# Transposed down products in three chunks of the last MoE stage: fp32r passes over split values instead of fp32 products

## The chip, the cores and the metric

The kernel runs on one core of one Trainium2 chip. The metric is the device time of one execution in microseconds. The kernel before takes 651.67 us, the median of three runs (651.1 to 653.26).

## What is computed

The input x holds 2 x 1024 tokens with 128 features. Six blocks are added to it one after another: a quantized FFN, a linear attention, the same FFN again, a mixture of experts (MoE), a causal softmax attention, and the same MoE a second time. Each block works on the layer-normed x. The change touches the last of them:

```
x = x + 0.5 * _L1_ffn_ref(_layernorm(x, axis=-1), ...)

logits = einsum('td,ed->te', x, router_w)          # 16 experts
top_w, top_i = top_k(softmax(logits), 2); top_w = top_w / sum(top_w)
dense_w = zeros((T, 16)).at[arange(T)[:, None], top_i].add(top_w)
for wg, wu, wd, cw in (Wg, Wu, Wd, dense_w.T):     # F = 64 each
    h = silu(x @ wg) * (x @ wu)
    acc = acc + cw[:, None] * (h @ wd)
shared = sigmoid(x @ shared_gate_w) * (silu(x @ Sg) * (x @ Su) @ Sd)   # FS = 256
```

All experts are computed for all tokens, and the weights of the experts not chosen are zero.

## The kernel before

**Units and chunks.** The 2048 tokens are cut into NC = 4 chunks of 512. The 16 x 64 expert columns and the 256 shared ones make NU = 10 units of 128 hidden columns. A MoE stage is a loop over 40 pairs of chunk and unit, numbered n = 0 to 39 in this text. Unit n of a chunk is u = n mod 10. `MOE0` is the first such stage and `MOE1` the last; both run the same code.

**What a unit does.** TensorE forms the gate and the up product of the unit (`gate_up`, L1325 to L1327): each is three fp32r passes of 512 columns over values that were split into a high and a low part (`mm3`), into banks 1 to 3 and 4 to 6 by turns. ScalarE takes Silu of the gate bank (L764, into `sg`). VectorE multiplies it with the up bank (L1130, into `su`) and that with the routing weights `gb` (L1134, into `hbuf`, three buffers by turns). Then TensorE does the down product of the unit: four products, one for each tile of 128 tokens, with the tile of `hbuf` as the stationary operand and 128 columns of the fp32 down weights `dw` as the moving one (L1545), summed over the ten units in bank 7 (`ACC`).

**Order on TensorE.** In step n of the loop in `moe` TensorE does gate_up(n), then at certain u the chunk's side work, then the down product of unit n - 2. The first three gate_up of the last stage are issued at the end of `causal`. gate_up(n) waits until `hbuf` of unit n - 3 is written, since it takes over that unit's banks.

**Side work of a chunk,** by u. At u = 1 TensorE transposes the next chunk's normed tokens into bank 0 (`ln`, L1333), ScalarE copies them out (L656), and VectorE adds the finished sum of the chunk before to x (`update`, L949) and splits the next chunk (`split`, L938 and L939). At u = 2 VectorE norms a later chunk (L925). At u = 3 TensorE forms the router's products (`route`, L1483 and L1485), which need that split, and VectorE picks the two experts. At u = 4 VectorE computes their weights (`weigh`). At u = 6 TensorE transposes them (`weights`, L1493), ScalarE copies them out (L752), and SyncE writes them to HBM. Bank 0 is passed from one of these users to the next: TensorE waits until the one before was drained (`t_take`).

**SyncE's queue.** For each chunk SyncE waits for the routing weights, writes them (L420), waits until they have landed, and then loads each unit's rows into `gb`, two loads a unit, 128 KB in all by the profile's count, four buffers by turns (L431). Behind the last of a chunk's loads stands the store of the finished chunk before (L436), which waits for `update`. The next chunk's L420 stands behind that store.

**GpSimd** has two short steps of the norm in this stage (L463, L464) and nothing else.

## Time and profile before

| | us |
|---|---|
| median of 3 runs | 651.67 |
| the profiled execution | 651.54 |
| its span | 649.8 |
| last MoE stage, from its first gate_up to the end of the span | 542.9 to 649.8 |
| TensorE busy over the span | 92% |
| VectorE busy over the span | 73% |
| GpSimd busy over the span | 25% |

The span is the time from the first to the last instruction; 1.7 us of the execution lie around it. TensorE carries the last stage nearly without a gap. The matmul records overlap each other, so that the duration of one record (0.40 us for 512 columns) is more than what it adds to the chain; the chain of work that ended last gives the distance from one to the next.

### The profile page before, as it was taken

Reading aid. Unit: us, or ns where it says so; the run is one execution under the profiler, and the core shown is the slowest. Engines: PE = TensorE matmul, PEld = TensorE weight load, DVE = VectorE, ACT = ScalarE, POOL = GpSimd, SP = SyncE. Lnnn points to the kernel's source line nnn. Section 1 sums busy time; section 2 is a strip of 40 time slices with the busy share of each in tenths; the row PEclk is TensorE's granted clock in tenths of the full one; section 3 lists DMA queues with packets and bytes.
Section 4 is the critical chain, followed back from the end, with each engine's and each line's share of the span. In section 5 each row is a group of like instructions: output and inputs, shape, how many; then the busy total and the mean of one; then the engine's idle time right before and its main releaser. Section 6 shows DMA issues by size and latency. Waiting matters only on the chain. (4 is left out here: it accounts for less than half of the span.)

```text
span 649.8 us, 12519 instructions
## 1 busy us (share of the span) xinstructions
PE 598.2 (92%) x4364; PEld 421.8 (65%) x4364; DVE 476.7 (73%) x1501; ACT 348.1 (54%) x713; POOL 161.4 (25%) x334
## 2 busy tenths in 40 slices
PE   6996879989999978999999999999999997999997
PEld 5785767878877956654535453545453545888887
DVE  5577866688787767879797878788879432976864
ACT  3855456323324552667676767676767674232321
POOL 7641534020024436722323121211120100000000
PEclk9999899999989995979999999999999999899999
DMA  8000000234322300000000000000000002333332
GB/s 297 6 2 0 2 1 0 68 101 131 116 75 79 94 1 2 1 2 1 2 2 2 1 3 1 1 2 2 1 3 1 2 2 68 99 121 126 115 126 71
DMA packets 18669, 27.98 MB, mean 43 GB/s; under 512 B 2984, under 2 KB 7208, under 8 KB 18608
## 3 DMA queue, kind: packets, MB, share of 16 engines
q1 hardware_dynamic: 17888, 25.85, 12.3%
q10 hardware_dynamic: 720, 1.34, 0.6%
q8 instruction: 35, 0.57, 0.4%
q14 instruction: 26, 0.21, 0.1%
HBM read 25.85 MB, written 1.33 MB: 42 GB/s over the span
## 5 line engine op out<-in xcount | busy, mean ns | idle before, releaser
L834 ACT ACTIVATE arena<-bank 128x512 f32<-128x512 f32 (+3 forms) x384 | 166.2, 496 | 66.5 <-PE bank L1669 46.1
L1700 PE MATMUL bank<-kza,qta 64*128 64x512 f32 (+3 forms) x432 | 139.5, 426 | 5.4 <-DVE work L1207 3.5
L1204 DVE CUSTOM_DVE_ANT_0 bank<-bank,mask_qk 128x512 f32<-128x512 f32 (+3 forms) x256 | 119.3, 518 | 32.1 <-PE bank L1700 31.7
L1657 PE MATMUL bank<-qtb,kza 64*128 64x512 f32 (+3 forms) x384 | 133.5, 407 | 4.4 <-ACT arena L834 1.6
L1700 PEld LDWEIGHTS bank<-kza,qta 64*128 64x128 f32 x432 | 69.3, 198 | 76.5 <-DVE work L1204 38.8
L764 ACT ACTIVATE work<-bank 128x512 f32<-128x512 f32 x80 | 47.7, 598 | 109.2 <-PE bank L1327 107.2
L1207 DVE TENSOR_REDUCE work<-bank 128x1 f32<-128x512 f32 x128 | 80.2, 683 | 15.5 <-PE bank L1700 15.5
L1545 PE MATMUL bank<-dw,work 128*128 128x128 f32 x640 | 86.2, 279 | 2.6 <-DVE work L1134 2.6
L1130 DVE TENSOR_TENSOR work<-work,bank 128x512 f32<-128x512 f32 x80 | 54.7, 683 | 44.3 <-PE bank L1327 39.8
L1545 PEld LDWEIGHTS bank<-dw,work 128*128 128x128 f32 x640 | 82.3, 193 | 7.2 <-issue 3.1
L1657 PEld LDWEIGHTS bank<-qtb,kza 64*128 64x128 f32 x384 | 64.6, 186 | 28.9 <-ACT arena L834 16.9
L1614 PE MATMUL bank<-arena 128*9 128x512 f32 (+3 forms) x768 | 80.8, 493 | 0.4 <-ACT arena L834 0.4
L1134 DVE TENSOR_TENSOR work<-work,kt 128x512 f32<-128x512 f32 x80 | 56.2, 703 | 5.1 <-DMA kt<-cw_rows 2.3
L463 POOL TENSOR_SCALAR rtmp<-mv 128x4 f32<-128x4 f32 x24 | 7.4, 308 | 170.5 <-DVE mv L913 170.1
L530 POOL CAST kza<-kt 32x512 fp32r<-32x512 f32 x48 | 29.1, 606 | 82.3 <-PE bank L1657 77.7
L1669 PE MATMUL bank<-identb,mask_kq 64*128 64x64 bf16 x512 | 47.6, 197 | 0.0
L925 DVE TENSOR_SCALAR hn<-x,mv,rs 128x128 f32<-128x128 f32 x96 | 29.0, 367 | 18.5 <-POOL rs L480 14.5
L1325 PE MATMUL bank<-qta,gh 128*128 128x512 f32 x80 | 38.4, 480 | 0.0
L1204 DVE DVE_READ_ACCUMULATOR2_ANT work<- 128x1 f32 x256 | 35.9, 140 | 0.0
L1377 PEld LDWEIGHTS bank<-work 128*128 128x128 f32 x256 | 32.4, 191 | 1.8 <-ACT work L674 0.3
L1377 PE MATMUL bank<-work 128*128 128x128 f32 x256 | 33.4, 275 | 0.1
L1669 PEld LDWEIGHTS bank<-identb,mask_kq 64*128 64x128 bf16 x512 | 24.6, 96 | 13.1 <-issue 8.2
(204 smaller groups left out, 1040.5 us busy)
## 6 DMA issues: line engine op xcount, KB each, us to landing
kt<-cw_rows SPq DMA_DIRECT2D x160, 128.0 KB, 2.9
x<-x_in SPq DMA_DIRECT2D x4, 256.0 KB, 7.4
y_out<-x SPq DMA_DIRECT2D x4, 256.0 KB, 3.2
arena<-gw_in SPq DMA_DIRECT2D x1, 640.0 KB, 9.6
arena<-uw_in SPq DMA_DIRECT2D x1, 640.0 KB, 8.6
dw<-dw_in SPq DMA_DIRECT2D x1, 640.0 KB, 9.5
work<-q_in SPq DMA_DIRECT2D x2, 256.0 KB, 8.0
arena<-const_in ACTq DMA_DIRECT2D x1, 400.0 KB, 6.7
```

The lines of the kernel that those rows point to most:

```text
L764: act.activation(sg[:, m % 2, :], bank[1 + m % 3][:, :], ACT.Silu).then_inc(sg_ready, 1)
L834: act.activation(pb[:, blk % 2, h, 0:w], s_bank(n)[:, 0:w], ACT.Exp, scale=SCALE).then_inc(p_ready, 1)
L1130: link(dve.tensor_tensor(su[:, m % 2, :], sg[:, m % 2, :], bank[4 + m % 3][:, :], ALU.mult))
L1134: dve.tensor_tensor(hbuf[:, m % 3, :], su[:, m % 2, :], gb[:, m % 4, :], ALU.mult)\
L1204: ins = dve.tensor_tensor_reduce(out=src, in0=src, in1=mask_qk[:, CW - w:], scale=1.0, scalar=-3e38, op0=ALU.add, op1=ALU.max, accum_out=dst)
L1207: ins = dve.tensor_reduce(dst, src, AX.X, ALU.max)
L1377: ins = pe.matmul(ACC[:, t * P:(t + 1) * P], hbuf[:, m % 4, t * P:(t + 1) * P], w2[:, k, :], start=False, stop=(k == FB - 1), skip_group_c ...
L1545: ins = pe.matmul(ACC[:, t * P:(t + 1) * P], hbuf[:, m % 3, t * P:(t + 1) * P], dw[:, u, :], start=(u == 0 and t == 0), stop=(u == NU - 1) ...
L1614: ins = pe.matmul(bank[7][h * SL:h * SL + HD + 1, CW - w:CW], va[:, b, j, g * GH + h, :], pb[:, blk % 2, h, 0:w], start=(j == 0), stop=Tru ...
L1657: ins = pe.matmul(s_bank(n)[:, 0:w], kz(s, h, j // CT)[pair(h), j % CT * P:(j % CT + 1) * P], qtb[pair(h), s % 2, (c + 1) * CW - w:(c + 1) ...
L1669: ins = pe.matmul(s_bank(n)[:, a * 2 * SL:(a + 1) * 2 * SL], mask_kq[r, a, :], identb[r, r], start=False, stop=True, skip_group_check=True)
L1700: ins = pe.matmul(a_bank(n)[:, 0:w], qta[pair(h), slot(b, g), i * P:(i + 1) * P], kz(s, h, half)[pair(h), 0:w], start=True, stop=True)
```

## The change

In the last MoE stage the down products of the first three chunks (units 0 to 29, `TURNED` = 30) take another form. The down weights become the stationary operand and the gated values the moving one, so that the sum arrives transposed, and both are split: three fp32r passes of 512 columns a unit in place of four fp32 products of 128 columns.

- `halves` splits the down weights once on VectorE (two passes of 128x1280), in step 7 of the causal stage.
- `high` copies each unit's gated values as their high part into `hhi` on ScalarE, behind the Silu of the next unit. GpSimd subtracts it from `hbuf` and writes the low part into `hlo`. Both have three buffers.
- `turned_down` does the three passes. It comes three steps behind gate_up instead of two, and so do the down products of the last chunk, whose form is the one of before.
- VectorE's write of `hbuf` for unit n waits until the low part of unit n - 3 is written, where it waited for the down product of that unit.
- At u = 2 of the next chunk ScalarE copies the transposed sum from bank 7 (`yturn`). At u = 7 TensorE transposes it back into bank 0 (`back`), and VectorE adds it to x from there. `update` of a chunk so moves from u = 1 to u = 7 of the next.
- The split weights, `hhi` and `hlo` lie in buffers of the causal stage, and the products that only keep TensorE busy at its end (`idle_product`) read another buffer.

```diff
@@ -617,7 +626,15 @@
             rstd(22)
-            rstd(23)
+            for n in range(TURNED):
+                pool.wait_ge(hhi_ready, n + 1)
+                if n >= 3:
+                    pool.wait_ge(down_done, 2 * NC * FB + NC * NU + n - 2)
+                pool.tensor_tensor(hlo[:, n % 3, :], hbuf[:, (NC * NU + n) % 3, :], hhi[:, n % 3, :].bitcast(F32),
+                                   ALU.subtract).then_inc(hlo_ready, 1)
+                if n == 4:
+                    rstd(23)
+                pool.wait_ge(hlo_ready, n + 1)
@@ -767,10 +784,24 @@
+                    if p == MOE1 and 1 <= n <= TURNED:
+                        high(n - 1)
+                    if p == MOE1 and c > 0 and u == 2:
+                        act.wait_ge(down_done, 2 * NC * FB + NC * NU + NU * c)
+                        if c > 1:
+                            act.wait_ge(back_full, c - 1)
+                        act.activation(yturn, ACC[:, :], ACT.Copy).then_inc(yt_copied, 1)
...
+            def high(n):
+
+                act.wait_ge(hm_ready, NC * NU + n + 1)
+                if n >= 3:
+                    act.wait_ge(down_done, 2 * NC * FB + NC * NU + n - 2)
+                act.activation(hhi[:, n % 3, :], hbuf[:, (NC * NU + n) % 3, :], ACT.Copy).then_inc(hhi_ready, 1)
@@ -1128,12 +1159,14 @@
-                    if m >= 3:
+                    if p == MOE1 and 3 <= n < TURNED + 3:
+                        dve.wait_ge(hlo_ready, n - 2)
+                    elif m >= 3:
                         dve.wait_ge(down_done, 2 * NC * FB + m - 2)
...
-                    if u == 1 and c > 0:
+                    if u == 1 and c > 0 and p == MOE0:
                         update(L - 1, 0.5)
@@ -1147,7 +1180,18 @@
+                    if p == MOE1 and c > 0 and u == 7:
+                        dve.wait_ge(back_full, c)
+                        update(L - 1, 0.5, T)
                 update(4 * p + 3, 0.5)
+
+            def halves():
...
+                link(dve.tensor_copy(dwh, flat))
+                dve.tensor_tensor(dwl, flat, dwh.bitcast(F32), ALU.subtract).then_inc(dws_ready, 1)
@@ -1518,7 +1564,8 @@
-                for n in range(NC * NU + 2):
+                lag = 3 if p == MOE1 else 2
+                for n in range(NC * NU + lag):
@@ -1535,16 +1582,42 @@
+                        if p == MOE1 and c > 0 and u == 7:
+                            back(L - 1, c)
+                    if p == MOE1 and lag <= n < TURNED + lag:
+                        turned_down(n - lag)
...
+            def turned_down(n):
...
+                if u == 0 and c > 0:
+                    pe.wait_ge(yt_copied, c)
+                pe.wait_ge(hlo_ready, n + 1)
+                f = slice(u * P, (u + 1) * P)
+                mm3(ACC[:, :], dwh[:, f], dwl[:, f], hhi[:, n % 3, :], hlo[:, n % 3, :], start=(u == 0),
+                    stop=(u == NU - 1)).then_inc(down_done, 1)
+
+            def back(L, c):
+
+                pe.wait_ge(yt_copied, c)
+                t_take(x_ready, L + 1)
+                for t in range(CT):
+                    ins = pe.transpose(T[:, t * P:(t + 1) * P], yturn[:, t * P:(t + 1) * P], ident[:, :])
+                ins.then_inc(back_full, 1)
```

TensorE at the start of the stage, before: the down product of unit 0 (bank 7 from `dw`) stands ahead of gate_up(3).

```order
L1333 MATMUL bank0<-identr,hn 128x128 x4
L1545 MATMUL bank7<-dw,work 128x128 x4
L1325 MATMUL bank2<-qta,gh 128x512
L1326 MATMUL bank2<-kt,gl 128x512
L1327 MATMUL bank2<-kt,gh 128x512
L1325 MATMUL bank5<-qta,vh 128x512
L1326 MATMUL bank5<-kt,vl 128x512
L1327 MATMUL bank5<-kt,vh 128x512
L1483 MATMUL bank0<-wr,kt 128x36
```

The same place after the change, where `mm3` is at L1371 to L1373 and the router's products at L1529:

```order
L1379 MATMUL bank0<-identr,hn 128x128 x4
L1371 MATMUL bank2<-qta,gh 128x512
L1372 MATMUL bank2<-kt,gl 128x512
L1373 MATMUL bank2<-kt,gh 128x512
L1371 MATMUL bank5<-qta,vh 128x512
L1372 MATMUL bank5<-kt,vl 128x512
L1373 MATMUL bank5<-kt,vh 128x512
L1529 MATMUL bank0<-wr,kt 128x36
```

The down product of unit 0 has moved behind the router's products, and nothing of unit 0 stands between the transposes and these any more.

ScalarE in chunk 1, before: Silu of the units (L764), the copy of the transposed tokens (L656) and the routing weights (L752).

```order
L752 ACTIVATE cwt<-bank 17x512
L764 ACTIVATE work<-bank 128x512 x5
L656 ACTIVATE ft<-bank 128x512
L764 ACTIVATE work<-bank 128x512 x3
L745 ACTIVATE th<-dd 128x8
```

After the change Silu is L781, the copy of the tokens L673, `high` L804 and the copy of the transposed sum L793:

```order
L781 ACTIVATE work<-bank 128x512
L673 ACTIVATE ft<-bank 128x512
L804 ACTIVATE kza<-work 128x512
L781 ACTIVATE work<-bank 128x512
L804 ACTIVATE kza<-work 128x512
L793 ACTIVATE work<-bank 128x512
L781 ACTIVATE work<-bank 128x512
```

Behind each Silu there is now one `high`, and at u = 2 also the copy of the sum, which waits for TensorE.

GpSimd in the last stage, before: the norm's two steps for chunks 2 and 3, then the end of the program.

```order
L463 TENSOR_SCALAR rtmp<-mv 128x4
L464 TENSOR_TENSOR rs<-rtmp,nhalf 128x4
L463 TENSOR_SCALAR rtmp<-mv 128x4
L464 TENSOR_TENSOR rs<-rtmp,nhalf 128x4
L176 UNCONDITIONAL_BRANCH
```

After the change (L472 and L473 are the norm's steps, L633 the subtraction):

```order
L472 TENSOR_SCALAR rtmp<-mv 128x4
L473 TENSOR_TENSOR rs<-rtmp,nhalf 128x4
L633 TENSOR_TENSOR qtb<-work,kza 128x512 x5
L472 TENSOR_SCALAR rtmp<-mv 128x4
L473 TENSOR_TENSOR rs<-rtmp,nhalf 128x4
L633 TENSOR_TENSOR qtb<-work,kza 128x512 x25
```

Thirty subtractions of 128x512 have been added, each with two tensor inputs in SBUF.

## Rows read from the trace of the kernel before

**Rows 1.** Windows over two chunks, from one `weights` on TensorE to the next.
```profile
core 0: us, PE busy (x) PEld busy (x) DVE busy (x) ACT busy (x) POOL busy (x), PEclk, DMA share, GB/s
564.25:588.80 24.55, 24.55 (x158) 21.79 (x157) 19.75 (x54) 7.37 (x13) 0.00 (x0) 1.00 0.33 117
588.80:613.35 24.55, 24.55 (x158) 21.80 (x157) 18.07 (x48) 7.37 (x13) 0.00 (x0) 1.00 0.39 120
```

**Rows 2.** Chain that ended last, in order of time: start us, us, what.
```profile
559.70 0.89 PE bank L1545 x8
560.59 0.23 PE bank L1325
...
564.25 0.44 PE bank L1493 x4
```

**Rows 3.** Groups by line, last stage: count, busy us, mean ns, idle before, releasers.
```profile
L764 ACT ACTIVATE work<-bank 128x512 f32<-128x512 f32 x40 | 23.8, 598 | 61.2 <-PE bank L1327 60.0 <-DVE work L1134 1.2
```

**Rows 4.** VectorE in order of time, start of the stage, and TensorE's wait there.
```profile
552.19 0.68 DVE L1130 TENSOR_TENSOR work<-work,bank 128x512 f32<-128x512 f32 x1
552.42 1.53 PE L1545 MATMUL bank<-dw,work 128*128 128x128 f32 x8 [1.86 <-DVE work L1134]
...
563.81 0.68 DVE L1130 TENSOR_TENSOR work<-work,bank 128x512 f32<-128x512 f32 x1
```

**Rows 5.** Window just behind that wait, columns as in rows 1.
```profile
553.00:556.50 3.50, 3.50 (x14) 2.92 (x13) 3.43 (x8) 0.60 (x1) 0.00 (x0) 0.51 0.54 150
```

**Rows 6.** VectorE in order of time, units 10 to 20.
```profile
573.90 0.69 DVE L1130 TENSOR_TENSOR work<-work,bank 128x512 f32<-128x512 f32 x1 [0.86 <-PE bank L1327]
...
580.49 1.11 DVE L925 TENSOR_SCALAR hn<-x,mv,rs 128x128 f32<-128x128 f32 x4
...
587.20 0.68 DVE L1130 TENSOR_TENSOR work<-work,bank 128x512 f32<-128x512 f32 x1
...
589.63 0.69 DVE L1134 TENSOR_TENSOR work<-work,kt 128x512 f32<-128x512 f32 x1
...
599.18 0.69 DVE L1134 TENSOR_TENSOR work<-work,kt 128x512 f32<-128x512 f32 x1
```

**Rows 7.** Groups by line and shape: GpSimd's passes over two SBUF tensors.
```profile
L498 POOL TENSOR_TENSOR arena<-arena 128x256 f32<-128x256 f32 x4 | 2.9, 727 | 0.3
L587 POOL TENSOR_TENSOR wl<-arena,wh 128x786 fp32r<-128x786 f32 x1 | 1.9, 1864 | 0.0
```

**Rows 8.** GpSimd and VectorE side by side in the first MoE stage.
```profile
208.06 0.73 POOL L498 TENSOR_TENSOR arena<-arena 128x256 f32<-128x256 f32 x1
208.24 1.10 DVE L1134 TENSOR_TENSOR work<-work,kt 128x512 f32<-128x512 f32 x1
...
194.12 0.73 POOL L498 TENSOR_TENSOR arena<-arena 128x256 f32<-128x256 f32 x1
194.42 0.98 DVE L1134 TENSOR_TENSOR work<-work,kt 128x512 f32<-128x512 f32 x1
...
207.23 0.76 POOL L496 TENSOR_TENSOR arena<-arena,rope 128x128 f32<-128x128 f32 x2
207.51 0.69 DVE L1130 TENSOR_TENSOR work<-work,bank 128x512 f32<-128x512 f32 x1 [0.84 <-PE bank L1327]
```

**Rows 9.** SyncE's queue at the end of chunk 1, and its loads' landing time.
```profile
589.76 0.59 SPq L436 DMA_DIRECT2D y_out<-x  x1
590.40 0.35 SPq L420 DMA_DIRECT2D cw_rows<-cwt  x1
594.02 6.32 SPq L431 DMA_DIRECT2D kt<-cw_rows  x9
...
DMA to landing us min/median/max: 2.7/2.9/4.0
```

**Rows 10.** VectorE's gap before the stage, and a pass of 128x1280.
```profile
540.47 0.69 DVE L949 SCALAR_TENSOR_TENSOR x<-bank,x 128x512 f32<-128x512 f32 x1 [9.50 <-PE bank L1639]
...
L974 DVE TENSOR_TENSOR gl<-arena,gh 128x1280 fp32r<-128x1280 f32 x1 | 1.8, 1801 | 0.0
```

More of the change, by code:

```diff
@@ L69 @@
 QKV_ASIDE, KEYS_ASIDE = 6, 5
+TURNED = (NC - 1) * NU
 def schedule():
@@ L129, in schedule @@
     put("dve", 7, 6, "weigh", 20)
+    put("dve", 7, 8, "halves")
     for engine in ("pe", "act"):
@@ L266, in macaron @@
         stm = sb("stm", [P, 2, CT, GH, SL], F32R)
+        dwh = kza[:, 0:2, :, :].rearrange("p a r n -> p (a r n)")[:, 0:NU * P]
+        dwl = qta[:, G:G + 2, :].rearrange("p g t -> p (g t)")[:, 0:NU * P]
+        hhi = kza[:, 2:4, :, :].rearrange("p a r n -> p (a r) n")
+        hlo = qtb[:, :, :].rearrange("p g (a n) -> p (g a) n", a=2)
         raw_a = arena[:, 0:W_END]
@@ L286, in macaron @@
         mix = loc
+        yturn = hbuf[:, 3, :]
         yt = [work[:, o:o + 2 * D].rearrange("p (t d) -> p t d", t=2) for o in (0, 2 * D, 4 * CW, 4 * CW + 2 * D)]
@@ L329, in macaron @@
         down_done = sem("down_done")
+        dws_ready, hhi_ready, hlo_ready, yt_copied, back_full = (
+            sem("dws_ready"), sem("hhi_ready"), sem("hlo_ready"), sem("yt_copied"), sem("back_full"))
         lg_full, dd_ready, th_ready, cw_ready, cw_full, cwt_ready = (
@@ L1149, in moe @@
                         weigh(r0 + c + 1)
+                    if p == MOE1 and c > 0 and u == 7:
+                        dve.wait_ge(back_full, c)
+                        update(L - 1, 0.5, T)
                 update(4 * p + 3, 0.5)
+            def halves():
+                dve.wait_ge(b_full, (STEPS - 1) * NBLK * GH)
+                dve.wait_ge(mx_full, 2 * STEPS)
+                flat = dw[:, :, :].rearrange("p u d -> p (u d)")
+                link(dve.tensor_copy(dwh, flat))
+                dve.tensor_tensor(dwl, flat, dwh.bitcast(F32), ALU.subtract).then_inc(dws_ready, 1)
             def tiles(n):
@@ L1285, in causal @@
                                 negate(*todo[1:])
+                            if todo[0] == "halves":
+                                halves()
                 yout(STEPS - 1, 1)
@@ L1537, in moe @@
                             weights(r0 + c + 1)
-                    if n >= 2:
-                        c, u = divmod(n - 2, NU)
-                        m = m0 + n - 2
-                        if u == 0:
+                        if p == MOE1 and c > 0 and u == 7:
+                            back(L - 1, c)
+                    if p == MOE1 and lag <= n < TURNED + lag:
+                        turned_down(n - lag)
+                    elif n >= lag:
+                        c, u = divmod(n - lag, NU)
+                        m = m0 + n - lag
+                        if u == 0 and p == MOE1:
+                            pe.wait_ge(yt_copied, c)
+                        elif u == 0:
                             acc_take(4 * p + c)
@@ L1547, in moe @@
                         ins.then_inc(down_done, 1)
+            def turned_down(n):
+                c, u = divmod(n, NU)
+                if n == 0:
+                    pe.wait_ge(dws_ready, 1)
+                    acc_take(4 * MOE1)
+                if u == 0 and c > 0:
[5 more added lines that the diff above has]
+            def back(L, c):
+                pe.wait_ge(yt_copied, c)
+                t_take(x_ready, L + 1)
+                for t in range(CT):
+                    ins = pe.transpose(T[:, t * P:(t + 1) * P], yturn[:, t * P:(t + 1) * P], ident[:, :])
+                ins.then_inc(back_full, 1)
             def tiles(n, first=""):
@@ L1677, in idle_product @@
                     h = A_HEADS[order]
-                    pe.matmul(bank[4 + order][:, :], qta[pair(h), slot(B - 1, G - 1), 0:P],
+                    pe.matmul(bank[4 + order][:, :], kz(STEPS - 1, h, 0)[pair(h), 0:P],
                               kz(STEPS - 1, h, 0)[pair(h), :], start=True, stop=True)
```

## The prediction

> **What bounds the kernel now.** The change lies in the last MoE stage, so I read first the windows between two `weights` products of TensorE, which mark chunks of equal content. Both windows last 24.55 us, and TensorE is busy through both at full clock [rows 1]. The chain of waits there is TensorE alone: the down product of a unit adds 0.89 us, a pass of 512 columns 0.23 us [rows 2]. The other engines wait for TensorE: ScalarE's Silu stood idle 60.0 us for it [rows 3], VectorE 0.86 us before an ordinary unit [rows 6]. But VectorE is nearly as full: 19.75 and 18.07 us busy of 24.55 [rows 1]. Its load is uneven, with all side work in u = 1 to 4, and that is what matters below.
>
> Three stretches of VectorE show how little room there is. I number units 0 to 39.
>
> - Chunk 0: VectorE starts `su` of unit 1 at 552.19 and `su` of unit 5 at 563.81, which are 11.62 us without a gap [rows 4]. Its weights are ready then, and TensorE turns them at 564.25 [rows 2]: 0.4 us of room.
> - Chunk 1: from `su` of unit 10 (573.90) to `su` of unit 15 (587.20) are 13.30 us [rows 6]. TensorE turns the weights at 588.80 [rows 1]: 1.6 us of room.
> - Chunk 2 is alike, without the norm of 1.03 us (1.11 in the row, of which 0.08 overlap the next) [rows 6].
>
> **What TensorE saves.** Three passes of 0.23 are 0.69 us in place of 0.89 [rows 2]: 0.20 a unit, 5.9 us for 30 units. The three transposes back cost 0.44 each, as the four transposes of `weights` do [rows 2]: 1.3 us. If TensorE stayed the bound throughout, that would be -4.6 us. The third step of lag moves products but adds none: three down products in place of two stand behind the last gate_up, and nothing waits there for their values. By the Trainium skill (FP8 and Floating Point Precision, TensorE Precision Notes) a true fp32 product takes four passes, so that three would be 0.67 us of 0.89; that would save 6.7 us, and no row contradicts it by more than these 0.03 us a unit.
>
> **What hides, at no cost.** The two passes of 128x1280 of `halves` fall into VectorE's gap of 9.50 us before 540.47; the one that the trace has took 1.80 us [rows 10]. `high` puts 0.60 us a unit on ScalarE [rows 3], 18 us into 60 us of idle time; the Silu of the next unit queues behind it, but its gate bank is ready only a unit later. The copy of the transposed sum waits for the last turned product of its chunk, and the first of the next waits for the copy; between these two stands gate_up, 6 x 0.23 = 1.4 us, against 0.60 us and two handovers. VectorE's wait for `back` at u = 7 is answered in the same step, right behind gate_up.
>
> **What GpSimd adds.** Thirty subtractions of 128x512 with two SBUF inputs. The rows have 0.727 us for 256 columns and 1.864 for 786 [rows 7]; between them 512 columns take 0.727 + 256 x 2.145 ns = 1.28 us. GpSimd has over 2 us a unit for it, so as an engine it holds. By the Trainium skill (GPSIMD Engine Reference, Elementwise: side-by-side cycle accounting) 2048 columns take 4.497 us, which would make 1.12 us of 512. The same section keeps elementwise work on VectorE; by its price the sum below would be about 2 us smaller, at 655.
>
> **What that does to VectorE** is the step on which the sum rests. L1134 takes 0.69 us when GpSimd is quiet. It took 1.10 when it began 0.18 us into a two-input pass of GpSimd, and 0.98 when it began 0.30 us into one [rows 8]. In both cases it began in effect 0.14 us before the other's recorded end. L1130, which reads a PSUM bank, kept its 0.69 us beside such a pass [rows 8]. I read this as: passes of two SBUF inputs take turns. So a GpSimd pass of 1.28 us shuts VectorE's SBUF passes out for up to 1.14 us. Bounds: at most 1.14 us is lost a unit, when it starts together with L1134. At least 0.54 is lost while VectorE has no idle time, when all 0.60 us of an L1130 lie beside it. The two measured delays, 0.41 and 0.29 us, are half of a pass of 0.73, which would be 0.6 of 1.28; the middle of the bounds is 0.84. I take 0.7.
>
> **What it does to the routing rows.** `update` moves from u = 1 to u = 7. The store in SyncE's queue waits for it, and behind the store stand the next chunk's L420 and L431. Before, the store went out at 589.76, L420 0.64 us later, the first load 3.6 us after that, at 594.02, and the second load of a unit lands 0.6 + 2.9 us on, at 597.5; unit 20 needs it at 599.18 [rows 9, 6]. Afterwards, with L1134 of unit 16 at 589.63 [rows 6] as the mark: unit 17 comes 2.08 + 0.44 us later (six passes, three passes, and `weights`), its write and the update take 1.3, so x is ready at 593.5 and the rows land at 593.5 + 0.64 + 3.6 + 3.5 = 601.3. Unit 20 asks for them four units, `weights` and `back` later, at 598.8. They are 2.5 us late, and more when unit 17 itself is delayed, up to 1.14; I take 3.6, since unit 17 starts at GpSimd's turn. The same happens at unit 30, where no side work follows.
>
> **The sum,** by the moment at which TensorE turns a chunk's weights:
>
> - First chunk: 552.19 + 11.62 + five GpSimd passes x 0.7 + 0.3 for handovers = 567.6, against 564.25: +3.3 (bounds +2.4 and +5.6). TensorE alone would be there much earlier.
> - First to second: before, `su` of unit 10 came 573.90 - 564.25 = 9.65 us behind the first; with four turned products 8.85. Then VectorE's 13.30, less the idle 0.86 and the update of 0.60 that moved, is 11.84, plus five passes x 0.7 = 3.5, plus 0.15: 24.3 us. TensorE alone would need 24.55 - 2.0 = 22.6. So 24.3 against 24.55: -0.2 (bounds -1.0 and +2.0).
> - Second to third: 8.85 + 0.44 for `back`, 11.84 - 1.03 = 10.8, four passes x 0.7 = 2.8 (GpSimd is idle while the rows are missing), 3.6 for the rows, 0.15: 26.6 against 24.55: +2.1 (bounds +0.4 and +4.3).
> - Third to the end: seven turned products -1.4, two transposes back +0.9, the late rows of unit 30, of which a third `hbuf` in hand covers most, +1.0 at the most 2: +0.5 (bounds 0 and +1.3).
>
> Together +5.7 us (bounds +1.8 and +13.2). The profiled execution took 651.54 with a span of 649.8, 0.13 below the median; on the median I predict **657.3**. So the change is slower, although TensorE has less to do.
>
> **The rivals.**
>
> *TensorE stays the bound (faster).* GpSimd's passes slip into VectorE's idle time and beside L1130, and no L1134 is shut out. Then the first chunk ends where VectorE's 11.62 us end, at -0.3; the next are -2.0 and -1.5, since the late rows (9.3 + 10.8 + 2.5 + 0.15 = 22.8) stay below TensorE's 23.0; the last -0.5: -4.3, 647.4 us. For it speaks that L1130 was not delayed in rows 8; against it that both L1134 that began inside a GpSimd pass were, and that in u = 1 to 4 VectorE has no idle time. Chance 0.14.
>
> *Gain and loss cancel.* The turns are taken, at the lower bound of 0.54, and the rows come 2.5 us late only. That is the lower end of the sum, +1.8 or a little less: 651 to 653.5. Chance 0.18.
>
> *The clock falls too.* After TensorE's wait of 1.86 us at 552.42 [rows 4] the granted clock was 0.51, the level of 1.2 GHz, from 553.0 to 556.5 [rows 5]. The new waits are 2 to 4 us, once or twice a chunk. Three such stretches, in each of which some eight passes take 0.2 us more, would be 3 x 1.7 = 5 us more if TensorE is the last there: 662.4. Against it: behind such a wait VectorE, not TensorE, comes last. Chance 0.10.
>
> *The passes are not shorter.* The turned passes have the form of gate_up's, 128 rows and 512 columns, so I give this no chance of its own.
>
> **How the numbers follow.** The forecast, turns at about 0.7 us and late rows, has 0.58; its own range is 653.5 to 662. The two cases with both signs stand beside it. The range of 8 in 10 is 648.5 to 664.5: it leaves out half of the first rival and the upper end of the bounds. A difference of 0.3%, 2.0 us, is about what a measurement of this kernel can tell from none. Faster by more: 0.14. Within it: 0.18. Slower by more: 0.68.
>
> **What would show it.** In the profile of the changed kernel: the down product of a turned unit adds 0.69 us to the chain; L633 takes 1.28 us, and more where it waits; L1134 (now L1167) has a mean of 0.9 to 1.2 us over the stage instead of 0.69; TensorE waits for VectorE at `route` and at `weights` of each of the three chunks, some 2 to 4 us in all each; the load of unit 20 lands after VectorE asks for it, and the store goes out some 4 us later in its chunk than before. The prediction is wrong if L1134 keeps 0.7 us beside L633, or if TensorE is busy through the windows of chunks 1 and 2; then they last 22.6 and 23.0 us.

## The result, and the profile after

The changed kernel takes 661.98 us, the median of four runs (659.92 to 664.35), against 651.38 us for the kernel before, measured again beside it. The ratio is 1.0158, with a 95% interval from 1.0127 to 1.0189: the change costs some 10.6 us. The forecast was 657.3 us with a range up to 664.5, so the sign was right and the time was within the range, but the loss was nearly twice the 5.6 us forecast.

The profiled execution took 664.35 us, the longest of the four, with a span of 662.6. I compare by the last stage, which begins at the first gate_up, and cut it where TensorE starts to turn a chunk's weights (three such places). The starts are read from the timeline of TensorE. Where TensorE does not wait, a start there stands about 0.16 us ahead of the one in the chain, which rows 1 and 2 give (564.08 for 564.25).

| length in us | before | after | difference | forecast |
|---|---|---|---|---|
| gate_up(0) to first weights | 21.23 | 24.95 | +3.7 | +3.3 |
| first to second | 24.56 | 24.89 | +0.3 | -0.2 |
| second to third | 24.54 | 28.29 | +3.8 | +2.1 |
| third to the end | 36.62 | 36.81 | +0.2 | +0.5 |
| stage | 106.95 | 114.94 | +8.0 | +5.7 |

The windows over these pieces, and one over 4 us behind the second `weights` (columns as in rows 1):

```profile
547.66:572.61 24.95, 19.75 (x84) 15.35 (x80) 18.78 (x61) 10.18 (x17) 8.58 (x9) 0.79 0.27 88
572.61:597.50 24.89, 22.74 (x106) 18.43 (x106) 22.46 (x52) 13.27 (x24) 15.71 (x11) 1.00 0.37 108
597.50:625.79 28.29, 25.04 (x111) 19.92 (x111) 21.79 (x49) 13.17 (x24) 14.19 (x10) 0.94 0.33 104
598.00:602.00 4.00, 4.00 (x16) 3.14 (x14) 2.37 (x5) 2.22 (x4) 2.11 (x2) 0.57 0.18 66
```

Against rows 1, TensorE is idle for 2.15 us of the second window and 3.25 of the third, and VectorE is busy for 22.46 us where it was for 19.75. Whom TensorE waits for in the stage (the waits of PE: us in total, times, longest):

```profile
PE bank L1539 <- DVE cw L1151: 4.8, 3, 2.2
PE bank L1529 <- DVE qta L970: 3.1, 2, 1.8
PE bank L1371 <- DVE work L1167: 1.8, 1, 1.8
```

These are `weights`, `route` and gate_up(3), and each time VectorE comes last. The third is not new: before, the down product of unit 0 waited 1.86 us for VectorE at this place [rows 4]. The groups of VectorE over the stage, first before, then after (L1134 is now L1167, L1130 is L1161, L939 is L970, L1117 is L1148):

```profile
L1134 DVE TENSOR_TENSOR work<-work,kt 128x512 f32<-128x512 f32 x40 | 27.7, 692 | 1.4
L939 DVE TENSOR_TENSOR qta<-ft,kt 128x512 fp32r<-128x512 f32 x3 | 2.1, 693 | 0.1
L1117 DVE TENSOR_TENSOR oh<-oh,tw 128x64 f32<-128x64 f32 x6 | 1.1, 222 | 0.1
```

```profile
L1167 DVE TENSOR_TENSOR work<-work,kt 128x512 f32<-128x512 f32 x40 | 33.1, 826 | 9.3 <-DMA kt<-cw_rows 6.9 <-PE bank L1598 1.4
L1161 DVE TENSOR_TENSOR work<-work,bank 128x512 f32<-128x512 f32 x40 | 27.3, 681 | 8.5 <-PE bank L1373 7.7 <-ACT work L781 0.6
L1148 DVE TENSOR_TENSOR oh<-oh,tw 128x64 f32<-128x64 f32 x6 | 4.3, 758 | 0.1
L970 DVE TENSOR_TENSOR qta<-ft,kt 128x512 fp32r<-128x512 f32 x3 | 4.0, 1332 | 0.1
```

L1161, which reads a PSUM bank, kept its 0.68 us. Elementwise passes with all operands in SBUF became longer in the mean: L1167 from 0.69 to 0.83 us, L970 from 0.69 to 1.33, L1148 from 0.22 to 0.76. GpSimd's own passes became longer too: 1.27 us at the shortest, 1.45 in the mean.

```profile
L633 POOL TENSOR_TENSOR qtb<-work,kza 128x512 fp32r<-128x512 f32 x30 | 43.6, 1452 | 35.2 <-ACT kza L804 32.0 <-issue 2.1 <-POOL qtb L633 0.3
```

What that does can be followed in the timelines of GpSimd and VectorE in chunk 0:

```profile
557.82 3.13 POOL L633 TENSOR_TENSOR qtb<-work,kza 128x512 fp32r<-128x512 f32 x2 [0.53 <-ACT kza L804]
563.63 1.36 POOL L633 TENSOR_TENSOR qtb<-work,kza 128x512 fp32r<-128x512 f32 x1 [2.68 <-ACT kza L804]
567.47 1.29 POOL L633 TENSOR_TENSOR qtb<-work,kza 128x512 fp32r<-128x512 f32 x1 [2.49 <-ACT kza L804]
570.91 1.29 POOL L633 TENSOR_TENSOR qtb<-work,kza 128x512 fp32r<-128x512 f32 x1 [2.15 <-ACT kza L804]
```

```profile
557.00 0.68 DVE L1161 TENSOR_TENSOR work<-work,bank 128x512 f32<-128x512 f32 x1
...
558.32 1.51 DVE L969 CAST kt<-ft 128x512 fp32r<-128x512 f32 x1
559.86 1.63 DVE L970 TENSOR_TENSOR qta<-ft,kt 128x512 fp32r<-128x512 f32 x1
...
564.48 1.06 DVE L1167 TENSOR_TENSOR work<-work,kt 128x512 f32<-128x512 f32 x1
...
567.74 0.17 DVE L1129 FIND_INDEX8 ix<-m,lg 128x8 uint32<-128x16 f32 x1
...
568.26 0.53 DVE L1130 TENSOR_TENSOR dd<-m 128x4 f32<-128x4 f32 x1
...
570.84 1.45 DVE L1148 TENSOR_TENSOR oh<-oh,tw 128x64 f32<-128x64 f32 x2
...
572.47 0.68 DVE L1161 TENSOR_TENSOR work<-work,bank 128x512 f32<-128x512 f32 x1
```

Each long pass of VectorE lies beside a subtraction. Not every pass beside one is long: FIND_INDEX8, which also works in SBUF, kept its 0.17 us beside the subtraction that begins at 567.47. The next elementwise pass, L1130, paid instead, with 0.53 us for 0.14. From `su` of unit 1 to `su` of unit 5 VectorE needs 572.47 - 557.00 = 15.47 us in place of 11.62 [rows 4]. The excess of 3.85 us lies in five places: 1.09 in the CAST, 0.94 in L970, 0.37 in L1167, 0.39 in L1130 and 1.09 in the pair of L1148.

The routing rows of chunk 2 in the timelines of SyncE's queue and VectorE, to be held against rows 9:

```profile
604.01 0.42 SPq L445 DMA_DIRECT2D y_out<-x  x1
604.48 0.35 SPq L429 DMA_DIRECT2D cw_rows<-cwt  x1
608.37 4.41 SPq L440 DMA_DIRECT2D kt<-cw_rows  x6
```

```profile
612.03 0.69 DVE L1167 TENSOR_TENSOR work<-work,kt 128x512 f32<-128x512 f32 x1 [2.77 <-DMA kt<-cw_rows]
...
614.04 1.32 DVE L1167 TENSOR_TENSOR work<-work,kt 128x512 f32<-128x512 f32 x1 [0.73 <-DMA kt<-cw_rows]
```

The store goes out 6.5 us behind the second `weights`, where it went 1.1 behind it before (589.76 against 588.64), and units 20 and 21 wait 2.77 and 0.73 us for their rows.

### The profile page after: what moved, and what is told of

Read it like the earlier page. It is cut to its first block and busy times, and to the rows that moved or that the text cites. A ratio compares the mean times of both kernels' runs of the same rounds, so it can differ in the third digit from the quotient of the medians.

```text
span 662.6 us, 12374 instructions
## 1 busy us (share of the span) xinstructions
PE 600.9 (91%) x4226; PEld 415.8 (63%) x4226; DVE 491.4 (74%) x1503; ACT 365.9 (55%) x746; POOL 204.5 (31%) x364
## 3 DMA queue, kind: packets, MB, share of 16 engines
HBM read 25.85 MB, written 1.33 MB: 41 GB/s over the span
## 5 line engine op out<-in xcount | busy, mean ns | idle before, releaser
L781 ACT ACTIVATE work<-bank 128x512 f32<-128x512 f32 x80 | 47.5, 595 | 78.3 <-PE bank L1373 74.8
L1161 DVE TENSOR_TENSOR work<-work,bank 128x512 f32<-128x512 f32 x80 | 54.6, 682 | 33.0 <-PE bank L1373 27.7
L1167 DVE TENSOR_TENSOR work<-work,kt 128x512 f32<-128x512 f32 x80 | 61.7, 771 | 13.0 <-DMA kt<-cw_rows 9.2
L472 POOL TENSOR_SCALAR rtmp<-mv 128x4 f32<-128x4 f32 x24 | 7.4, 307 | 163.6 <-DVE mv L944 163.3
L1598 PE MATMUL bank<-dw,work 128*128 128x128 f32 x400 | 53.9, 281 | 0.8 <-DVE work L1167 0.8
L633 POOL TENSOR_TENSOR qtb<-work,kza 128x512 fp32r<-128x512 f32 x30 | 43.6, 1452 | 35.2 <-ACT kza L804 32.0
L1598 PEld LDWEIGHTS bank<-dw,work 128*128 128x128 f32 x400 | 51.6, 195 | 2.9 <-issue 1.0
L1371 PE MATMUL bank<-qta,gh 128*128 128x512 f32 x80 | 36.5, 456 | 1.8 <-DVE work L1167 1.8
```

Source lines behind the costliest of these rows:

```text
L1161: link(dve.tensor_tensor(su[:, m % 2, :], sg[:, m % 2, :], bank[4 + m % 3][:, :], ALU.mult))
L1167: dve.tensor_tensor(hbuf[:, m % 3, :], su[:, m % 2, :], gb[:, m % 4, :], ALU.mult)\
L1371: pe.matmul(dst, ah, bl, start=start, stop=False)
L1598: ins = pe.matmul(ACC[:, t * P:(t + 1) * P], hbuf[:, m % 3, t * P:(t + 1) * P], dw[:, u, :], start=(u == 0 and t == 0), stop=(u == NU - 1) ...
```

## Experiments

Two causes were forecast together: GpSimd's passes and VectorE's take turns (turns), and the routing rows come late (rows). The first experiments take one away, then the other, then both. Each piece of the stage is given as in the table above.

### The same kernel again

> The changed kernel itself, a second time. The last stage, from its first gate_up to the end of the span, was 107.0 us in the profile of before and 114.9 in that of after; the whole was 10.6 us slower. If the change costs only in that stage, its length comes back within 0.5 us and the two falls of the granted clock ahead of it (200 to 204 and 492 to 500 us) lie elsewhere or are absent; the ratio is then about 1.013. If something of the change slows the stages ahead, the same delay stands at the same places again and the ratio is 1.016 or more.

Measured: 667.8 us (665.33 to 668.98, four runs), 1.0218 (1.0175 to 1.0261) against before. The pieces are 24.86, 24.90, 31.47 and 37.04. The same program is 5.8 us slower here than above, and the kernel before, measured beside it, is 1.9 us slower too (653.29). The stage did not come back within 0.5 us as expected: it is 118.27 us, 3.3 more than above, and 3.2 of that lie in the third piece. The ratio is over the 1.016 that was to show a delay ahead of the stage, but the falls of the clock did not come back at 200 to 204 and 492 to 500 us: it is 1.00 in both. The windows of this kernel there, behind a wait of TensorE of 2.77 us at `route` that ends at 618.89:

```profile
614.50:618.90 4.40, 1.63 (x7) 1.04 (x7) 4.33 (x5) 2.68 (x5) 2.98 (x2) 0.98 0.60 190
618.90:624.90 6.00, 6.00 (x18) 5.13 (x19) 4.66 (x20) 1.84 (x4) 1.75 (x2) 0.50 0.27 88
```

TensorE was busy for 1.63 us of 4.40, and then ran at the level of 1.2 GHz for six. So the price of the change is not one number: what a wait costs depends on whether the clock falls behind it. Later differences of less than 3 us between kernels with such waits are read from the pieces, not from one median.

### GpSimd's work taken away

```diff
-                pool.tensor_tensor(hlo[:, n % 3, :], hbuf[:, (NC * NU + n) % 3, :], hhi[:, n % 3, :].bitcast(F32),
-                                   ALU.subtract).then_inc(hlo_ready, 1)
+                pool.tensor_tensor(hlo[:, n % 3, 0:8], hbuf[:, (NC * NU + n) % 3, 0:8],
+                                   hhi[:, n % 3, 0:8].bitcast(F32), ALU.subtract).then_inc(hlo_ready, 1)
```

> GpSimd subtracts only 8 of the 512 columns of each unit, so that the low part of the gated values is left out but for these; all waits and all else stay. Turns theory (a two-input pass of GpSimd shuts VectorE's SBUF passes out): L1167 is back at 0.69 us, the weights of chunk 0 are turned 21 us behind the first gate_up instead of 24.9, windows of chunks 1 and 2 are 22.6 and 23.0 us, the stage about 103 us and the whole 647 to 649. Rival (the late routing rows are the main cost): the window of chunk 2 stays at 26 us or more and the whole at 655 or more. Second rival (the longer hand-over over ScalarE and GpSimd is what delays, not the port): the whole gains only the 1.1 us a unit by which the subtraction is shorter where someone waits for it, and L1167 keeps passes of over 1 us.

Measured: 650.76 us (ten runs), 0.9967 (0.994 to 0.9994). The pieces are 21.56, 22.53, 24.27 and 36.76. This kernel leaves out nearly all of the low part, so it is a probe and no complete version. With the same waits, the same lag and the same copies, but passes of 0.30 us, the stage is 9.8 us shorter than that of the change, and the median 11.2 us lower (17.0 against the same kernel again). The first piece is nearly that of before again, and the second is what TensorE alone was forecast to need (22.6). The third is 1.3 us above the 23.0 expected, and the whole 1.8 above the expected range. So the number of hand-overs from VectorE by ScalarE and GpSimd to TensorE does not carry the loss. This run alone does not part a GpSimd pass that shuts VectorE out from one that TensorE only waits for longer; the run with contention alone, below, does. VectorE over the stage:

```profile
L1167 DVE TENSOR_TENSOR work<-work,kt 128x512 f32<-128x512 f32 x40 | 27.7, 692 | 9.7 <-DMA kt<-cw_rows 7.2 <-PE bank L1598 1.4
```

### The stores moved behind the next chunk's rows

```diff
             for r in range(2 * NC):
                 combine_weights(r)
-                if r > NC:
-                    store(r - NC - 1)
+                if r > NC + 1:
+                    store(r - NC - 2)
+            store(NC - 2)
             store(NC - 1)
```

> In SyncE's queue the store of a finished chunk goes behind the routing rows of the next chunk, so that no load waits for update at u = 7. Turns theory: only the late rows go away, 2.8 + 0.7 us of VectorE's waiting in chunk 2, so the window of chunk 2 falls from 28.3 to about 25.5, the rest stays, the whole is 2.5 to 3.5 us faster than the changed kernel, 658 to 660. Rows theory: the stage falls to 108 us or less and the whole to 654 or less.

> Both edits (8 of 512 low columns only, and the store later in SyncE's queue). Turns theory: as the light kernel, or up to 0.5 us faster, since late rows alone hide behind TensorE: stage 102.5 to 103.5 us, whole 646.5 to 649. Rows theory: this one is at 647 to 649 while the light kernel alone is at 653 or more.

Measured with the full subtraction: 660.24 us (five runs), 1.0122 (1.0064 to 1.018), pieces 24.86, 24.89, 26.29 and 36.77. Only the third piece moves, by -2.0 us, to 26.29 where 25.5 was expected: VectorE waits for rows for 0.4 us in all, not 6.9. Measured with the light one: 648.83 us (seven runs), 0.9939 (0.9915 to 0.9963), pieces 21.44, 22.57, 23.01 and 36.69. Its windows:

```profile
566.83:589.40 22.57, 22.57 (x107) 18.52 (x106) 18.71 (x53) 13.12 (x25) 3.10 (x11) 1.00 0.39 123
589.40:612.41 23.01, 23.01 (x112) 18.91 (x111) 18.28 (x49) 13.07 (x25) 2.50 (x10) 1.00 0.38 119
```

With both causes gone TensorE is busy throughout, for 22.57 and 23.01 us. These are the 22.6 and 23.0 that the forecast gave for TensorE alone, so its price for the turned products and for `back` holds in these two pieces. The third piece splits thus: the late rows are 1.3 us of it with quick passes (24.27 to 23.01) and 2.0 with long ones. The long passes are the other 3.3 (23.01 to 26.29). Half of these 3.3 us is not VectorE's turns but TensorE's clock: behind a wait of 2.22 us at the second `weights` it was 0.57 over 4 us, and `su` of unit 20 came 11.04 us behind `weights` instead of 9.47. That late rows alone would hide behind TensorE here, as expected, is not so: they cost the 1.3 us.

### VectorE's long pass freed from SBUF

A pass with an operand in PSUM was not delayed in the trace of before [rows 8]. So I let the product of Silu and up stay in its PSUM bank, and L1167 read it from there:

```diff
-                    link(dve.tensor_tensor(su[:, m % 2, :], sg[:, m % 2, :], bank[4 + m % 3][:, :], ALU.mult))
+                    prod = bank[4 + m % 3] if p == MOE1 else su[:, m % 2, :]
+                    link(dve.tensor_tensor(prod[:, :], sg[:, m % 2, :], bank[4 + m % 3][:, :], ALU.mult))
...
-                    dve.tensor_tensor(hbuf[:, m % 3, :], su[:, m % 2, :], gb[:, m % 4, :], ALU.mult)\
+                    dve.tensor_tensor(hbuf[:, m % 3, :], prod[:, :], gb[:, m % 4, :], ALU.mult)\
```

> The changed kernel, complete, with one edit in the last stage: VectorE writes the product of Silu and up back into the up product's PSUM bank instead of into su, so that the next pass (L1168 here) reads one SBUF tensor and one bank instead of two SBUF tensors. GpSimd's subtraction stays whole. Turns theory (two passes that each read two SBUF tensors take turns): the ordinary units are no longer shut out, the pass keeps 0.69 us beside GpSimd; only split, norm and weigh still take turns. Piece to the first weights 22 to 23.5 us (24.9 in the changed kernel, 21.2 before), window of chunk 1 22.6 to 23.2, of chunk 2 24 to 25, the whole 649 to 653. Rival (any SBUF access of VectorE waits for GpSimd, whatever the count of its inputs): no change, stage 113 to 118 us. Second rival (the longer hand-over is the cost): no change either.

> The same edit, and the store of a finished chunk behind the next chunk's routing rows in SyncE's queue. Turns theory: window of chunk 2 about 23.0 to 23.5 us, stage 104 to 105.5 us, the whole 0.2 to 0.6% faster than the kernel before. Rivals: stage 112 us or more.

Measured alone: 659.57 us (ten runs), 1.0104 (1.0086 to 1.0123), pieces 24.52, 24.30, 26.19 and 36.73. With the later stores: 654.88 us (ten runs), 1.005 (1.0016 to 1.0083), pieces 24.53, 24.25, 23.44 and 36.70. The expectations were missed by far: 649 to 653 us for the first and a stage of 104 to 105.5 for the second, which has 108.92. VectorE in the first of them:

```profile
L1168 DVE TENSOR_TENSOR work<-bank,kt 128x512 f32<-128x512 f32 x40 | 27.6, 691 | 9.7 <-DMA kt<-cw_rows 7.3 <-PE bank L1599 1.3
L970 DVE TENSOR_TENSOR qta<-ft,kt 128x512 fp32r<-128x512 f32 x3 | 4.0, 1332 | 0.1
L1148 DVE TENSOR_TENSOR oh<-oh,tw 128x64 f32<-128x64 f32 x6 | 3.2, 582 | 0.1
```

L1168 has one of its two inputs in PSUM and the other in SBUF, and takes its 0.69 us in all 40 passes, although some 22 of them overlap a subtraction. That a PSUM operand frees the pass is confirmed, and still the first piece shrinks by only 0.4 us. The side work with operands in SBUF keeps paying: L970 takes 1.33 us as before the edit, and the 128x64 products 0.58 instead of 0.22. In chunk 0 there was little to win, since L1167 had paid only 0.37 of the 3.85 us. That is gone and the CAST lost 0.64 us instead of 1.09, but L1130 lost 0.74 instead of 0.39: five subtractions cost 3.40 us (from `su` of unit 1 at 552.12 to `su` of unit 5 at 567.14, 15.02 us).

### Contention alone, on the kernel before

Thirty subtractions of two resident SBUF tensors into a buffer that nobody reads, released by VectorE's write of `hbuf` (in the change ScalarE's copy of it stands between). TensorE keeps its fp32 products.

```diff
-            rstd(23)
+            for n in range(3 * NU):
+                pool.wait_ge(hm_ready, NC * NU + n + 1)
+                pool.tensor_tensor(spare[:, :], qta[:, 4, 0:CW].bitcast(F32), qta[:, 5, 0:CW].bitcast(F32),
+                                   ALU.subtract).then_inc(spare_done, 1)
+                if n == 4:
+                    rstd(23)
...
```

> The kernel before, complete, with nothing of the change but a load on GpSimd: behind each of the first 30 units of the last stage it subtracts two SBUF tensors of 128x512 that nobody waits for. Turns theory: the pass that writes hbuf and the side work of VectorE are shut out in u = 1 to 4; piece to the first weights 21.2 -> 23 to 25 us, windows of chunks 1 and 2 24.55 -> 25 to 27, the whole 4 to 8 us slower. Rival (the cost is in the hand-over or in the late rows): GpSimd's work is waited for by nobody, so the stage stays at 107.0 us.

Measured: 662.98 us (four runs), 1.0136 (1.0053 to 1.0218), pieces 24.68, 29.49, 27.08 and 36.55: the stage is 10.8 us longer, although nobody waits for GpSimd. The 10.3 us of the median are more than the 4 to 8 expected, and the second piece is above its 25 to 27. VectorE over this stage:

```profile
L1142 DVE TENSOR_TENSOR work<-work,kt 128x512 f32<-128x512 f32 x40 | 32.3, 808 | 1.9 <-DMA kt<-cw_rows 0.6
L933 DVE TENSOR_SCALAR hn<-x,mv,rs 128x128 f32<-128x128 f32 x8 | 4.2, 587 | 0.0
L1121 DVE TENSOR_TENSOR oh<-iota,ixf 128x64 f32<-128x64 f32 x6 | 4.0, 699 | 0.1
```

Here the norm (0.34 us each before) and the first 128x64 product are hit, which the change left alone. Which of these passes pays depends on where the subtraction falls. Not all of the 10.8 us is contention. Behind TensorE's waits of 3.19 and 2.10 us at the first two `weights` its clock was lower:

```profile
568.58:572.58 4.00, 4.00 (x16) 3.55 (x15) 2.66 (x4) 1.03 (x2) 2.40 (x2) 0.50 0.30 80
598.07:602.07 4.00, 4.00 (x18) 3.63 (x17) 2.66 (x4) 1.19 (x2) 2.40 (x2) 0.62 0.34 110
```

VectorE's `su` of units 10 and 20 came 12.50 and 11.44 us behind `weights`, where it comes 9.82 behind in the kernel before. That is 4.3 us, so by my estimate some 6.5 us are left for the turns themselves.

### Late rows alone, on the kernel before

```diff
             def store(c):
                 sp.wait_ge(x_ready, 4 * MOE1 + c + 1)
+                if c < 2:
+                    sp.wait_ge(hm_ready, NC * NU + NU * (c + 1) + 8)
```

> The kernel before, complete, with one more wait in SyncE's queue: the stores of chunks 0 and 1 wait until unit 17 (27) has written hbuf, about when the changed kernel has its update. The rows of unit 20 then land at about 600.7 us instead of 597.5, 1.5 us after VectorE asks for them. Turns theory: TensorE has 1.6 us of room at the weights, so the window of chunk 2 stays within 0.5 us of 24.55 and the whole within 0.3%: late rows alone cost nothing, they cost where VectorE is already late. Rows theory: window of chunk 2 3 us longer, the whole 3 us or more slower.

Measured: 654.93 us (ten runs), 1.0035 (1.0002 to 1.0068), pieces 21.24, 24.55, 25.65 and 37.58. The stage is 2.1 us longer, 1.1 in the third piece and 1.0 in the last. I had expected at most 0.5 us in the third piece. So late rows cost something even with nothing on GpSimd, about half of their waits of 4.4 us. TensorE's waits show where:

```profile
PE bank L1547 <- DVE x L951: 1.7, 2, 0.9
```

The first down product of chunks 2 and 3 waits for `update`, which empties bank 7 and which VectorE does only behind the late pass of unit 21 or 31. The changed kernel empties bank 7 on ScalarE, so it has no such wait, and the price of late rows there is the 1.3 to 2.0 us found above. They are the smaller cause, neither the whole loss nor nothing.

### A finer grain on GpSimd

Each subtraction in two passes of 256 columns, or four of 128:

```diff
-                pool.tensor_tensor(hlo[:, n % 3, :], hbuf[:, (NC * NU + n) % 3, :], hhi[:, n % 3, :].bitcast(F32),
-                                   ALU.subtract).then_inc(hlo_ready, 1)
+                for q in range(2):
+                    w = slice(q * 256, (q + 1) * 256)
+                    ins = pool.tensor_tensor(hlo[:, n % 3, w], hbuf[:, (NC * NU + n) % 3, w],
+                                             hhi[:, n % 3, w].bitcast(F32), ALU.subtract)
+                ins.then_inc(hlo_ready, 1)
```

> The changed kernel, complete, with GpSimd's subtraction cut into two passes of 256 columns. Turns theory: a pass shuts VectorE out for at most 0.6 us instead of 1.14, and VectorE gets its turn between the halves. The about three long collisions a chunk (1.0 us each) shrink to about half: piece to the first weights 24.9 -> 23.5 to 24.3, window of chunk 1 24.9 -> 23.5 to 24.3, the whole 1.5 to 4 us faster than the changed kernel. Rival (the total time of GpSimd's passes counts, not their grain): each half costs 0.73 us, so the pair is 0.15 to 0.2 us longer, and nothing gets faster.

> Product of Silu and up in the PSUM bank, the store behind the next chunk's rows, and GpSimd's subtraction in two passes of 256 columns. What still takes turns is the split's subtraction and weigh, 1.0 us each in the kernel with the first two edits (pieces 24.5, 24.25, 23.4). Turns theory: each falls to about 0.5 us or less: pieces about 23.3, 23.2, 23.1 us, stage 106 to 106.5 us, the whole within 0.3% of the kernel before. Rival (grain without effect): stage 109 us again.

> As that one, with four passes of 128 columns (about 0.4 us each, 1.6 us a unit). Turns theory: a collision costs at most 0.3 us: pieces 22.5, 22.8, 23.0, stage about 105 us, if GpSimd's 1.6 us a unit still fit in TensorE's 2.08. Rival (GpSimd itself becomes late, since each of its passes now waits for a turn): TensorE waits at the turned products for hlo, windows of 23.5 us or more.

Halves alone: 660.13 us (ten runs), 1.0089 (1.0053 to 1.0126), pieces 24.26, 25.44, 28.61 and 36.92, a stage of 115.23 us where the change has 114.94. Nothing is gained, where 1.5 to 4 us were expected: a pass is shorter, but there are now twice as many to meet. The norm of a chunk, four SBUF passes in a row that take 1.11 us [rows 6], took 2.97 here:

```profile
581.42 5.41 POOL L635 TENSOR_TENSOR qtb<-work,kza 128x256 fp32r<-128x256 f32 x6 [0.97 <-POOL qtb L635]
```

```profile
583.94 2.97 DVE L959 TENSOR_SCALAR hn<-x,mv,rs 128x128 f32<-128x128 f32 x4
```

With the PSUM operand and the later stores, halves gave 655.08 us (twelve runs), 1.0034 (0.9995 to 1.0072), pieces 23.21, 24.97, 23.60 and 36.77; the second was expected at 23.2, and the whole is no faster than with whole passes (654.88). Quarters gave 652.3 us (ten runs), 0.9978 (0.9944 to 1.0012), pieces 23.04, 23.25, 23.23 and 36.78, a stage of 106.30 where about 105 was expected. GpSimd and the split in the latter:

```profile
L636 POOL TENSOR_TENSOR qtb<-work,kza 128x128 fp32r<-128x128 f32 x120 | 53.1, 474 | 17.2 <-issue 9.6 <-POOL qtb L636 4.1 <-ACT kza L808 2.7
```

```profile
L974 DVE TENSOR_TENSOR qta<-ft,kt 128x512 fp32r<-128x512 f32 x3 | 2.5, 832 | 0.1
```

In the kernel with the same edits and whole passes GpSimd is busy for 39.6 us and the split's subtraction takes 1.66. Here GpSimd is busy for 53.1 us, but each turn is short, and the subtraction takes 0.83: it loses 0.14 us instead of 0.97.

### The split's subtraction from PSUM as well

To the kernel with the PSUM operand, halves and later stores, for the last stage:

```diff
-                dve.tensor_tensor(ul[:, tok(c)], src, uh[:, tok(c)].bitcast(F32), ALU.subtract)\
+                raw = T[:, :] if L > 20 else src
+                dve.tensor_tensor(ul[:, tok(c)], raw, uh[:, tok(c)].bitcast(F32), ALU.subtract)\
...
-                t_take(ft_ready, L + 1)
+                t_take(split_ready if L > 20 else ft_ready, L + 1)
```

> As the kernel in halves, and the split's subtraction reads the transposed tokens from PSUM bank 0 instead of their copy in SBUF, so that it too has one SBUF input. Turns theory: the subtraction takes 0.69 us in every chunk, the route no longer waits for it, each of the three pieces is up to 0.5 us shorter than in the kernel in halves: stage 104.8 to 106 us, the whole 0 to 0.4% faster than the kernel before. Rival: only passes of hbuf collide, the split's 1.67 us came from elsewhere and stays.

Measured: 652.67 us (twelve runs), 0.9974 (0.9942 to 1.0007), pieces 22.42, 23.70, 23.62 and 36.80. The first two pieces are 0.8 and 1.3 us shorter than in the same kernel without this edit, and the stage of 106.54 is half a microsecond over the expected range. TensorE no longer waits at `route`, and those at `weights` are 2.1 us where the change has 4.8:

```profile
PE bank L1545 <- DVE cw L1156: 2.1, 3, 1.0
```

```profile
L975 DVE TENSOR_TENSOR qta<-bank,kt 128x512 fp32r<-128x512 f32 x3 | 2.1, 692 | 0.1
```

These last two are the best complete versions. Their stages, 106.5 and 106.3 us, are half a microsecond shorter than that of before (106.95), but their times cannot be told from it. Of TensorE's saving of 4.6 us the light kernel with later stores keeps 3.2 in the stage (106.95 to 103.71). The 2.6 to 2.8 us between it and these two go to the full subtraction, in the main to what is left of the turns.

## Why the prediction was right, and where it was off

**TensorE's saving: right.** In the changed kernel's chain a turned product adds three pieces of 0.23 us, and with both causes removed the windows are 22.57 and 23.01 us, as forecast. The first piece gives nothing back, since VectorE bounds it.

**What hides: right.** The kernel with the PSUM operand has the same `halves` and the same work ahead of the stage, and starts it at 542.76, where before starts at 542.85. `high` took 0.63 us on ScalarE, and the light kernel shows that the hand-overs cost next to nothing (a first piece of 21.56 for 21.23).

**GpSimd's pass: 1.28 forecast, right for an undisturbed one** (1.27 to 1.30), but 1.45 in the mean. I had not counted that GpSimd is held up as well.

**The turns: the cause right, the size nearly, the victim partly wrong.** I put 0.7 us on each subtraction. In chunk 0 five of them cost 15.47 - 11.62 = 3.85 us, 0.77 each, and the first piece came out at +3.7 against +3.3. But I expected L1167 to pay it, with a mean of 0.9 to 1.2 us. It had 0.83, and in chunk 0 3.5 of the 3.85 us fell on the side work. That is why moving L1167's operand alone brought so little. My reading "passes of two SBUF inputs take turns" was also too narrow on one side: the CAST, and the norm in the run with contention alone, have one tensor input and paid, while FIND_INDEX8 did not.

**The late rows: right in sum, in part by luck.** The forecast had 3.6 us, of which 2.5 were the rows themselves; it was 2.77 for unit 20 and 0.73 for unit 21, 3.5 in all. But unit 20 asked 11.8 us behind `weights`, where 10.0 were reckoned, and had its rows 14.5 behind, where 12.5 were. Both were late by about the same, behind the same slow stretch (below), and so their distance stayed. From `su` of unit 20 to `su` of unit 25 the forecast is 10.8 + 2.8 + 3.6 = 17.2 us, and the trace has 625.65 - 608.57 = 17.1.

**The last piece: right by luck.** The forecast +0.5 holds two errors that cancel. With the third step of lag 17 down products stand behind the third `weights` instead of 16, which the sum left out: with the row's 0.89 us for it TensorE alone would come to +0.4 and not -0.5 (+0.1 was measured with both causes removed). And the late rows of unit 30 cost nearly nothing (36.81 with them, 36.77 with the later stores), not 1.0. Measured: +0.2.

**The step that failed** is the 8.85 + 0.44 = 9.3 us from the second `weights` to `su` of unit 20. It stood for TensorE at full clock, and the trace has 608.57 - 597.50 = 11.1, which is 1.8 of the 2.3 us by which the stage was missed. The profiles of seven kernels show why. TensorE's wait in front of the second `weights`, the granted clock in the 4 us that begin 0.5 us behind its start, and the time to `su` of unit 20:

| kernel | wait | clock | us to `su` 20 |
|---|---|---|---|
| after | 2.15 | 0.57 | 11.07 |
| the same again | 2.15 | 0.57 | 11.01 |
| later stores | 2.22 | 0.57 | 11.04 |
| PSUM operand | 1.55 | 1.00 | 9.56 |
| halves alone | 2.72 | 1.00 | 9.50 |
| PSUM operand, halves, later stores | 2.27 | 1.00 | 9.53 |
| light | none | 1.00 | 9.47 |

```profile
597.50 0.61 PE L1539 MATMUL bank<-identr,cw 128*17 128x128 f32 x4 [2.15 <-DVE cw L1151]
...
599.22 0.63 PE L1372 MATMUL bank<-kt,gl 128*128 128x512 f32 x1
```

The passes behind the wait are recorded with 0.63 us instead of 0.40. At full clock the stretch takes 9.5 to 9.6 us behind a wait (the 9.47 of the light kernel, without one, are the forecast 9.3 in the chain's count), so 1.5 of the 1.8 us are the clock. The length of the wait alone does not decide whether it falls: halves alone waited longest and kept full clock. What does decide stays open. Its window behind the wait:

```profile
594.67:598.67 4.00, 4.00 (x22) 3.17 (x21) 3.57 (x7) 2.10 (x4) 2.36 (x3) 1.00 0.20 74
```

The rival "the clock falls too" named this, at 1.7 us for each stretch, and got a chance of only 0.10 because VectorE would come last behind such a wait. In u = 5 to 9 there is no side work, and there TensorE is the bound again: it has no gap from 597.50 to `su` of unit 20. So the forecast's mechanism and this rival were both at work. I had treated them as exclusive, and left the second out of the sum.

**What stays open** is the rest, some 2.6 us between the stage's +8.0 and the medians' +10.6. In the profiled execution the stage starts 4.8 us later than before, at 547.66. Part of it are two stretches ahead of the stage, first of the kernel before and then of the changed one:

```profile
200.00:204.00 4.00, 4.00 (x29) 3.52 (x28) 2.26 (x6) 1.85 (x4) 0.24 (x1) 1.00 0.30 86
492.00:500.00 8.00, 7.92 (x59) 3.49 (x63) 6.61 (x13) 5.75 (x11) 0.00 (x0) 1.00 0.00 0
```

```profile
200.00:204.00 4.00, 4.00 (x22) 3.58 (x21) 0.33 (x1) 1.19 (x3) 0.29 (x1) 0.68 0.27 98
492.00:500.00 8.00, 8.00 (x35) 2.84 (x34) 4.50 (x8) 4.02 (x8) 0.00 (x0) 0.57 0.00 0
```

The program is nearly the same there, and the falls stand elsewhere in other profiles: the same kernel again has full clock from 492 to 500 and starts the stage at 547.93 all the same. A late start of the stage also comes without the change: the kernel before with late stores, whose program is that of before up to this stage, starts it at 546.78. The ten other profiles with the change start it anywhere from 542.65 to 547.93. So one profile's 4.8 us cannot be put down to the change. Whether it makes such falls more frequent, with one profile for each kernel, stays open.

## What to carry to other kernels

Elementwise work moved to GpSimd takes time from VectorE's elementwise passes wherever both have all operands in SBUF, even if nobody waits for GpSimd. Price it by how full VectorE is in that stretch, here 0.77 us for each pass of 1.28 where VectorE has no gap. Leaving an operand in PSUM frees a VectorE pass from it, but the turn can then fall on another SBUF pass, so every pass of the stretch has to be counted. And where the change makes TensorE wait anew, as here for 2.15 to 2.77 us, price the work behind the wait at the lower clock as well, as a case with a chance of its own: waits of 2.27 and 2.72 us were also followed by full clock.

## What the hardware showed that was not expected

- A VectorE pass with one input in PSUM and one in SBUF, writing to SBUF, was never delayed by GpSimd: 40 passes at 0.69 us in each of the five profiles that have it, some 22 of them beside a subtraction in the first.
- The delay does not follow the size of the delayed pass: two products of 128x64 took 1.45 us beside a subtraction (before, 0.22 each), and a CAST with a single input took 1.51 where 0.42 is its time before. All 12 FIND_INDEX8 passes of the stage lie beside a subtraction, and their mean of 0.17 us is that of before. GpSimd is delayed in turn: two subtractions took 3.13 us, against 2 x 1.28.
- Four passes of 128 columns keep GpSimd busy for 1.77 us (120 passes, 53.1 us), one of 512 for 1.32 (39.6 us for 30), and yet the stage was 2.6 us shorter with them (106.30 against 108.92, both with the PSUM operand and the later stores).
- The same program had medians of 661.98 and 667.8 us in two sets of four runs, 0.9% apart, while each set kept within 0.7% and the kernel before moved by 0.3% (651.38 and 653.29).
